# Two attention heads at a time on the two row halves of TensorE, in the expert layers of a four-layer kernel

## The reference

```python
    def _L0_ffn_ref(x, ln1_g, ln1_b, ln2_g, ln2_b, wq, bq, wk, bk, wv, bv, wo, bo, gate_w, gate_b, w1, b1, w2, b2):
        B, S, H, NH, E, F = (4, 128, 128, 16, 8, 512)
        D = H // NH
        ...
        b, s, h = x.shape
        hn = _layernorm(x, ln1_g, ln1_b)
        q = (hn @ wq + bq).reshape(b, s, NH, D).transpose(0, 2, 1, 3)
        ...
        scores = jnp.einsum('bhqd,bhkd->bhqk', q, k) / jnp.sqrt(jnp.float32(D))
        attn = jax.nn.softmax(scores, axis=-1)
        o = jnp.einsum('bhqk,bhkd->bhqd', attn, v)
        o = o.transpose(0, 2, 1, 3).reshape(b, s, h)
        x = x + (o @ wo + bo)
        hn2 = _layernorm(x, ln2_g, ln2_b).reshape(-1, h)
        logits = hn2 @ gate_w + gate_b
        idx = jnp.argmax(logits, axis=-1)
        ...
    x = x + _L0_attn_a_ref(_layernorm(x, axis=-1), ...)
    x = x + _L0_ffn_ref(_layernorm(x, axis=-1), ...)
    x = x + _L0_attn_b_ref(_layernorm(x, axis=-1), ...)
    x = x + _L0_ffn_ref(_layernorm(x, axis=-1), ...)
    return x
```

## Time and profile before

| | us |
|---|---|
| median of 3 runs | 1390.95 (1387.69 to 1395.62) |
| the profiled execution, its own time | 1389.94 |
| its span, first to last instruction | 1388.0 |
| PE busy | 1160.6 (84%) |
| VectorE busy | 982.9 (71%) |
| ScalarE busy | 689.2 (50%) |
| mean granted TensorE clock | 0.908 |

### The profile page before, as it was taken

The page is one execution under the profiler, slowest core; times in us unless marked ns, Lnnn a source line. Parts: engine busy times, 40 slices in busy tenths (PEclk is TensorE's granted clock), DMA queues, the critical chain, the costliest instruction groups (busy, mean ns, idle before and its releaser), DMA issues. The chain is left out here.

```text
span 1388.0 us, 33225 instructions
## 1 busy us (share of the span) xinstructions
PE 1160.6 (84%) x13034; PEld 628.2 (45%) x13034; DVE 982.9 (71%) x2128; ACT 689.2 (50%) x1425; POOL 618.8 (45%) x828
## 2 busy tenths in 40 slices
PE   6746777769999998887787988969988999999885
PEld 2212332323333334864465666656666433333375
DVE  5699999978888984535856665736725688888453
ACT  3843443414776767532452452442441367676744
POOL 2359989964235312531632452442532243342153
PEclk9969889987999999898998878989978799999988
DMA  5288944131241402235132232141132303140223
GB/s 152 115 298 315 344 171 172 56 79 49 45 98 53 118 4 88 66 96 107 29 88 51 44 82 55 31 103 28 32 82 47 72 2 92 44 126 10 86 59 89
DMA packets 132800, 127.65 MB, mean 92 GB/s; under 512 B 86295, under 2 KB 117847, under 8 KB 128122
## 3 DMA queue, kind: packets, MB, share of 16 engines
q1 hardware_dynamic: 124592, 117.65, 30.0%
q0 software_dynamic: 2496, 5.13, 1.2%
q10 hardware_dynamic: 5558, 2.76, 1.0%
HBM read 104.83 MB, written 37.90 MB: 103 GB/s over the span
## 5 line engine op out<-in xcount | busy, mean ns | idle before, releaser
L1480 DVE TENSOR_REDUCE f_row_min<-f_ps 128x1 f32<-128x512 f32 x480 | 308.1, 681 | 54.5 <-PE f_ps L1811 54.0
L1361 ACT ACTIVATE f_e<-f_ps 128x512 f32<-128x512 f32 x512 | 279.1, 598 | 124.9 <-PE f_ps L1830 124.1
L816 PE MATMUL m_ps<-m_shared,sb_ident 128*128 128x512 f32 x256 | 132.5, 663 | 54.9 <-DVE m_shared L664 52.9
L379 POOL TENSOR_TENSOR m_drive<-m_du,m_ring 128x1024 f32<-128x1024 f32 x64 | 149.7, 2354 | 49.0 <-DVE m_ps L656 31.7
L522 ACT ACTIVATE m_ps<-m_delta,m_A 128x511 f32<-128x511 f32 x128 | 82.9, 681 | 117.2 <-DVE m_ps L656 98.3
L1841 PE MATMUL f_ps<-f_e,f_v_op 128*32 128x512 f32 x1024 | 137.3, 608 | 2.4 <-ACT f_e L1361 1.4
L2700 DVE TENSOR_REDUCE d_row_min<-d_ps 128x1 f32<-128x384 f32 (+3 forms) x176 | 104.2, 632 | 23.1 <-PE d_ps L2935 22.0
L816 PEld LDWEIGHTS m_ps<-m_shared,sb_ident 128*128 128x128 f32 x256 | 51.2, 211 | 138.5 <-DVE m_shared L664 81.6
L656 DVE TENSOR_TENSOR_SCAN m_ps<-m_ps,m_drive 128x1024 f32<-128x1024 f32 x44 | 101.1, 2297 | 5.0
L1811 PE MATMUL f_ps<-f_second_ops 72*128 72x512 bf16 x256 | 98.0, 383 | 2.8 <-DVE f_row_min L1480 2.8
L1811 PE MATMUL f_ps<-first_ops 72*128 72x512 bf16 x224 | 92.2, 421 | 8.6 <-DVE f_row_min L1480 6.4
(11 more groups left out here) (319 smaller groups left out, 2305.5 us busy)
## 6 DMA issues: line engine op xcount, KB each, us to landing
m_ring<-bc_scr SPq DMA_DIRECT2D x32, 1024.0 KB, 5.4
f_rows_scr<-blank SPq DMA_DIRECT2D x2, 8707.5 KB, 32.0
f_wall<-f_wall SPq DMA_DIRECT2D x16, 578.0 KB
first_ops<-q_scr SPq DMA_DIRECT2D x28, 288.0 KB
first_ops<-k_scr SPq DMA_DIRECT2D x84, 96.0 KB
f_second_ops<-q_scr SPq DMA_DIRECT2D x16, 288.0 KB
f_second_ops<-k_scr SPq DMA_DIRECT2D x48, 96.0 KB
f_second_ops<-f_rows_scr SPq DMA_DIRECT2D x36, 64.5 KB, 1.8
```

Of the source, the lines that this page charges most:

```text
L379: nc.gpsimd.tensor_tensor(drive[:, step % AHEAD, :].rearrange("p (a s) -> p a s", a=HALVES), du[:, :, tokens(b)], b_row(step).unsqueeze(1) ...
L816: last = nc.tensor.matmul(bank(Y + k), core.ident[:, :], hC[:, k * S:(k + 1) * S], start=False, stop=last_of_batch)
L1361: nc.scalar.activation(e_sb[:, n % 3, hh, :], ps[:, SCORE[(b * UNITS + u) % SCORE_BANKS], :], ACT.Exp, scale=SCALE).then_inc(s["e_out"], 1)
L1480: nc.vector.tensor_reduce(row_min[:, b % 2, u // TPB, u % TPB:u % TPB + 1], ps[:, MAXQ[unit(b, u) % MAX_BANKS], :], AX.X, ALU.max, negate= ...
```

## The change

For batches 1 to 3 of each expert layer (batch 0 stays as it is) a head no longer has its rows at partitions 0 to 71. Two heads are put side by side: head A has 64 of its 72 rows at partitions 0 to 63, head B 64 of its rows at 64 to 127. These 64 rows hold all products of parts but the last, third query part by third key part. That product's 8 rows and the 3 shift rows, 11 rows, stand at the head of the same half, in another slot of the same tensor (`REST_AT` heads further on).

- A maximum uses the 64 rows alone: one matmul per unit as before, on one row half; two units of two heads follow each other (`placed_head`).
- A score becomes two matmuls into one bank: 64 rows, then 11 rows. TensorE's program has, for a pair: 64 rows of A, 64 rows of B, 11 rows of A, 11 rows of B. Only the last one of each tells ScalarE.
- In the whole loop, batch 0 too, two maxima follow each other and then two scores.
- Loading a group of heads takes 12 DMAs (48, 16 and 8 rows, query and key, two halves) instead of 4, with 2 KB pieces instead of 4 KB and the same bytes. A quarter's shifts take two DMAs instead of one, and batch 2 also reloads ones, one DMA per group. On SyncE groups 2 and 3 of a batch are now loaded behind the shifts of quarter 3.

```diff
+HALF = P // 2
+LOW_ROWS = (PARTS - 1) * PARTS * HD
+REST_AT = GROUP // 2
...
                 def load_group(b, g):
                     if b >= 2:
                         sp.wait_ge(s["s_ps"], (b - 2) * UNITS + (g + 1) * GROUP * TPB)
-                    heads = slice(g * GROUP, (g + 1) * GROUP)
-                    sp.dma_start(q_op(b, slice(0, QK_ROWS))[:, heads, :], query_rows(q_scr[stored(b), :, :, heads, :])).then_inc(
-                        op_in[b % 2][g], 16)
-                    load_keys(b, g, heads)
+                    ops = second_ops if b % 2 else core.first_ops
+                    at, rest_at = slice(g * GROUP, g * GROUP + REST_AT), slice(g * GROUP + REST_AT, (g + 1) * GROUP)
+                    for half in range(2):
+                        heads = slice(g * GROUP + half * REST_AT, g * GROUP + (half + 1) * REST_AT)
+                        rows = halves(ops)[half]
+                        for i, (low, high, rest) in enumerate((some_query_rows(q_scr[stored(b), :, :, heads, :]),
+                                                               some_key_rows(k_scr[stored(b), :, :, heads, :]))):
+                            sp.dma_start(rows[0:LOW_ROWS, i, at, :], low).then_inc(op_in[b % 2][g], 16)
+                            sp.dma_start(rows[LOW_ROWS:HALF, i, at, :], high).then_inc(op_in[b % 2][g], 16)
+                            sp.dma_start(rows[0:HD, i, rest_at, :], rest).then_inc(op_in[b % 2][g], 16)
...
                 def for_maximum(b, u):
-                    hd, t, n = u // TPB, u % TPB, unit(b, u)
+                    hd, t, half, slot = placed_head(b, u)
+                    n = unit(b, u)
...
-                    nc.tensor.matmul(ps[:, MAXQ[n % MAX_BANKS], :], q_op(b, QK)[:, hd, t * P:(t + 1) * P],
-                                     k_op(b, QK)[:, hd, :], start=True, stop=True).then_inc(s["max_ps"], 1)
+                    rows, slot = (slice(0, QK_ROWS), hd) if b == 0 else (slice(half * HALF, (half + 1) * HALF), slot)
+                    nc.tensor.matmul(ps[:, MAXQ[n % MAX_BANKS], :], q_op(b, rows)[:, slot, t * P:(t + 1) * P],
+                                     k_op(b, rows)[:, slot, :], start=True, stop=True).then_inc(s["max_ps"], 1)
...
-                    if n >= SCORE_BANKS:
-                        pe.wait_ge(s["e_out"], n - SCORE_BANKS + 1)
-                    hd = g * GROUP + hh
-                    nc.tensor.matmul(ps[:, SCORE[n % SCORE_BANKS], :], k_op(b, QKS)[:, hd, t * P:(t + 1) * P],
-                                     q_op(b, QKS)[:, hd, :], start=True, stop=True).then_inc(s["s_ps"], 1)
+                    cols = slice(t * P, (t + 1) * P)
+                    for p in range(2):
+                        if n + p >= SCORE_BANKS:
+                            pe.wait_ge(s["e_out"], n + p - SCORE_BANKS + 1)
+                        bank = ps[:, SCORE[(n + p) % SCORE_BANKS], :]
+                        if b == 0:
+                            hd = g * GROUP + u % GROUP + p
+                            nc.tensor.matmul(bank, k_op(b, QKS)[:, hd, cols], q_op(b, QKS)[:, hd, :],
+                                             start=True, stop=True).then_inc(s["s_ps"], 1)
+                        else:
+                            rows, slot = slice(p * HALF, (p + 1) * HALF), g * GROUP + u % GROUP // 2
+                            nc.tensor.matmul(bank, k_op(b, rows)[:, slot, cols], q_op(b, rows)[:, slot, :],
+                                             start=True, stop=False)
+                    for p in range(2 if b else 0):
+                        rows, slot = slice(p * HALF, p * HALF + HD + PARTS), g * GROUP + REST_AT + u % GROUP // 2
+                        nc.tensor.matmul(ps[:, SCORE[(n + p) % SCORE_BANKS], :], k_op(b, rows)[:, slot, cols],
+                                         q_op(b, rows)[:, slot, :], start=False, stop=True).then_inc(s["s_ps"], 1)
...
-                    if m < B:
+                    if m < B and mu % 2 == 0:
                         for_maximum(m, mu)
-                    if 0 <= b < B:
-                        score(b, u)
+                        for_maximum(m, mu + 1)
+                    if 0 <= b < B and u % 2 == 0:
+                        scores(b, u)
```

More of the change, by code:

```diff
@@ L933 @@
 STEPS = GROUPS * TPB
+HALF = P // 2
+LOW_ROWS = (PARTS - 1) * PARTS * HD
+REST_AT = GROUP // 2
+HALF_LOADS = 6
 SCORE_BANKS = 3
@@ L1056, in k_op, with halves, in_slots, placed_head @@
             return (second_ops if b % 2 else core.first_ops)[rows, 1]
+        def halves(ops):
+            return [ops[half * HALF:(half + 1) * HALF] for half in range(2)]
+        def in_slots(rows, first):
+            return rows.rearrange("r (g e a) s -> r g e a s", g=GROUPS, e=2)[:, :, first // REST_AT, :, :]
+        def placed_head(b, u):
+            if b == 0:
+                return u // TPB, u % TPB, None, None
+            g, v = divmod(u, GROUP * TPB)
+            a, v = divmod(v, 2 * TPB)
+            return g * GROUP + v % 2 * REST_AT + a, v // 2, v % 2, g * GROUP + a
+        def head_in_group(b, p):
+            return p if b == 0 else p % 2 * REST_AT + p // 2
         skipped_units, skipped_quarters, skipped = (ENTERED, ENTERED_QUARTERS, 1) if entered else (0, 0, 0)
@@ L1067, in shifts_loaded @@
         def shifts_loaded(b, k):
[L1068 removed]
+            return 16 * 2 * (b + 1 - (k < skipped_quarters))
         def operand_loads(b, g):
[L1071 to L1074 removed]
+            first = 0 if b % 2 or entered or g < KEY_GROUPS else PARTS
+            ones = 1 if b == 2 else 0
+            return 16 * (first + ones + 2 * HALF_LOADS * ((b + 1) // 2))
         def prepared_at(m):
@@ L1278, in shifts @@
                     sp.wait_ge(s["m_out"], quarter(b, k) + 1)
-                    sp.dma_start(q_op(b, slice(QK_ROWS, SHIFT_ROWS))[:, quarter_heads(k), :].rearrange("j h (t s) -> j (h t) s", t=TPB),
-                                 max_part[:, k, :]).then_inc(m_in[k], 16)
+                    for half in range(2):
+                        heads = slice(k * GROUP + half * REST_AT, k * GROUP + (half + 1) * REST_AT)
+                        rest_at = slice(k * GROUP + REST_AT, (k + 1) * GROUP)
+                        rows = (q_op(0, slice(QK_ROWS, SHIFT_ROWS))[:, heads, :] if b == 0 else
+                                halves(second_ops if b % 2 else core.first_ops)[half][HD:HD + PARTS, 0, rest_at, :])
+                        sp.dma_start(rows.rearrange("j h (t s) -> j (h t) s", t=TPB),
+                                     max_part[half * PARTS * IN_QUARTER // 2:(half + 1) * PARTS * IN_QUARTER // 2, k, :]).then_inc(
+                            m_in[k], 16)
                 def load_walls(first):
@@ L1291, in _ @@
                         load_keys(0, g, slice(g * GROUP, (g + 1) * GROUP))
-                for o in range(skipped, 2):
-                    sp.dma_start(k_op(o, slice(QK_ROWS, SHIFT_ROWS)),
-                                 core.dram["ones"].rearrange("j (h s) -> j h s", h=NH)).then_inc(s["ones_in"], 16)
+                ones = core.dram["ones"].rearrange("j (h s) -> j h s", h=NH)
+                if not skipped:
+                    sp.dma_start(k_op(0, slice(QK_ROWS, SHIFT_ROWS)), ones).then_inc(s["ones_in"], 16)
+                for rows in halves(second_ops):
+                    sp.dma_start(in_slots(rows[HD:HD + PARTS, 1], REST_AT), in_slots(ones, REST_AT)).then_inc(s["ones_in"], 16)
                 for b in range(B):
@@ L1298, in _ @@
                             shifts(b, k)
-                    if skipped < b + 1 < B:
+                    goes_on = skipped < b + 1 < B
+                    if goes_on:
                         store_parts(b + 1)
-                        for g in range(GROUPS // 2):
-                            load_group(b + 1, g)
-                    shifts(b, 2)
-                    if skipped < b + 1 < B:
-                        for g in range(GROUPS // 2, GROUPS):
-                            load_group(b + 1, g)
-                    shifts(b, 3)
+                        load_group(b + 1, 0)
+                    shifts(b, 2)
+                    if goes_on:
+                        load_group(b + 1, 1)
+                    shifts(b, 3)
+                    for g in range(2, GROUPS):
+                        if goes_on:
+                            load_group(b + 1, g)
                     if b >= 1:
@@ L1816, in turn_maxima, with scores @@
                     pe.wait_ge(*side_free("maxima", b, k))
-                    nc.tensor.matmul(ps[0:PARTS * IN_QUARTER, SIDE, 0:P], min_part[:, :, :].rearrange("p j r -> p (j r)"),
+                    nc.tensor.matmul(ps[0:PARTS * IN_QUARTER, SIDE, 0:P], min_part[:, :, :, :].rearrange("p e j r -> p (e j r)"),
                                      w["ident_b"], start=True, stop=True).then_inc(s["mT_ps"], 1)
-                def score(b, u):
-                    q, hh, n = u // GROUP, u % GROUP, b * UNITS + u
+                def scores(b, u):
+                    q, n = u // GROUP, b * UNITS + u
```

42 lines of the change are left out of this document (26 added, 16 removed).

## The result

The changed kernel takes 1432.94 us (median, 1427.49 to 1441.03), the kernel before beside it 1390.98: a ratio of 1.0323, 95% interval 1.0277 to 1.0368. That is 42 us slower; the forecast was 1424, its range 1392 to 1465. The profiled executions differ by 1427.49 - 1389.94 = 37.6, where the sum of the prediction has 34.8. The mean granted clock is 0.908 in both.

A forecast was written before the change was run, and what follows sets the result against it. TensorE was taken to bound the kernel. Per layer 17.2 - 8.3 + 2.3 + 5.2 + 1 = 17.4 us, twice 34.8, added to 1389.94 gave 1424.7, stated as 1424, with a range of 1392 to 1465.

The forecast's parts named there:

- Overlap: Pairs of matmuls on different row halves stream together, 0.22 us for two instead of 0.44, the second starting 0.03 later.
- tile change: On TensorE, each change between 64-row and 32-row tiles costs 0.09 us, within bounds of 0 and 0.16.
- loop: A pair's second score waits for ScalarE to free its bank: 1.39 us; clean step 3.27 against 2.84, end step 3.05.
- free changes: Rival: changing between 64-row and 32-row tiles on TensorE costs nothing; step 3.10 us, time 1400; chance 0.09.
- the loop doesn't hold TensorE back: Rival: results reach ScalarE sooner or the second score's bank is free when asked; step 2.52 to 2.76, time 1370; chance 0.09.
- 40 x 0.43, -8.3, 2.3, 5.2, 1: Terms in us per layer: steps beside maxima, waits filled by blocks, other blocks' tile changes, end steps, batch 0; sum 17.4.
- the term of 0.43 a step: Each of 40 score steps beside maxima in a layer becomes 0.43 us longer, 3.27 against 2.84; 17.2 per layer.
- Ten blocks at 0.09: Ten blocks of other work per batch each add one tile change of 0.09 us; 2.3 per layer.
- SyncE hidden in layer 3: In the second expert layer, four groups of loads at 5.4 us each end before quarter 2's shifts are wanted; no cost.
- the fourth rival: Rival: the forecast plus SyncE late, every issue costing 0.87 us, some 11 late in the second expert layer; 1437; chance 0.06.
- Groups 2 and 3, now behind quarter 3's shifts: nothing: On SyncE, these loads are wanted 32 and 48 units after their batch starts, so moving them costs nothing.
- TensorE sets the pace: In the kernel before, from batch 1's scores to batch 2's, TensorE is busy 55.69 of 57.82 us and is the bound.

The follow-up runs named there:

- e2: Changed kernel with both heads of a pair on rows 0 to 63, so no two matmuls overlap, and a smaller exponential scale; 1660.77 us.
- e1: Changed kernel with each 11-row matmul replaced by a second pass over the same 64 rows, and a smaller exponential scale; 1421.46 us, ratio 1.026.
- e10: Changed kernel with VectorE's maximum and, from the fourth step on, ScalarE's exponential reading 64 of 512 columns; 1398.38 us, ratio 1.009.
- e11: Kernel before with VectorE's maximum and ScalarE's exponential cut to 64 of 512 columns, the control of e10; 1363.47 us, ratio 0.983.
- e7: Changed kernel with batch 0's shifts issued ahead of the loads of groups 2 and 3 in the second expert layer; 1439.01 us, ratio 1.038.
- e5: Changed kernel with ScalarE's exponentials on 256 of 512 columns from the fourth step on; 1431.16 us, ratio 1.033.
- e9: Changed kernel unaltered, run again on the chip of e10 to e12; 1448.85 us, ratio 1.047 to the kernel before.
- e6: Kernel before with ScalarE's exponentials on half of the columns from the fourth step on; 1380.19 us, ratio 0.997.
- e3: Changed kernel with maxima still packed but each score one matmul of 75 rows, and a smaller exponential scale; 1406.11 us, ratio 1.015.
- e12: Changed kernel with the second 64-row pass of e1 and the 64-column readers of e10; 1381.73 us, ratio 0.996.

## Why the prediction was right

- **Overlap, tile change, loop.** Two 64-row matmuls stream in the time of one, the second at most 0.01 behind, not 0.03 (e2 without the overlap: 3.99 a step, as worked out). The change between 64 and 32 rows is 0.09, as taken; e1 removes it. The loop through ScalarE is 1.45 for 1.39, the clean step 3.30 for 3.27, the end step 3.10 for 3.05. The rivals "free changes" and "the loop doesn't hold TensorE back" fall; the second would have needed readers that e10 had to shorten to an eighth.
- **40 x 0.43, -8.3, 2.3, 5.2, 1.** In sum 17.4 against 16.8 in layer 1. That it comes so close is partly luck, as single terms are off in both directions. Batch 1 lost less (3.4 for 4.5): the kernel before already waited there, 3.2 us by e11, of which 0.8 ahead of its products, and the term of 0.43 a step takes a step without waits as the base. Batch 3 lost less (6.1 and 0.8 for 7.4). Batches 0 and 2 lost half a us more, in batch 2 through the wait of batch 3's first score.
- **Ten blocks at 0.09: mis-sized.** Leaving a 128-row tile costs more than going into a 32-column one: 0.59 for 0.43 at the turns, 0.99 for 0.81 at the logits, 1.3 us over batch 1's blocks where the term has 0.9, and 1.8 between e10 and e11. The Trainium skill, "TensorEngine Tiling (Array Packing)", Key Properties, has it that changing the tiling mode drains TensorE, with no figure; these runs agree, and the price depends on what is left: 0.09 from 64 rows to 32, 0.16 to 0.18 out of a block.
- **SyncE hidden in layer 3: this step failed.** I drew a line through issues of 3, 24 and 72 rows and read 0.38 for 16 rows; it is 0.60 to 0.70. A group is 7.1 to 7.2 us instead of 5.4, four of them and the ones put the shifts past their time, and batch 0 waits 3.5 us; e7 takes 3.9 us off by their order alone. It was the fourth rival's mechanism, at a third of its price.
- **"Groups 2 and 3, now behind quarter 3's shifts: nothing": this failed too.** I looked at when these loads are wanted and not at what stands behind them on SyncE, batch 3's first shifts. It costs 0.7 and 0.5 us in the changed kernel, and up to 3.3 us in the variants whose batches are shorter (e5).
- **The clock: "I expect 2.4 GHz to stay".** True in batch 1 of every run but e2, and in the first profile from batch 1 on. Not true in others: in e9 TensorE stands for 2 to 3 us and then has 7 and 17 us at 1.2 GHz. In the profiles this is 16.3 of the 19.1 us between two executions of the same kernel, and the likely difference between 1.032 and 1.047 on two chips. It is one reason why e5 and e7 can't be judged by their totals. I had given it no share; it belonged in the range's upper part.
- **"TensorE sets the pace"** was only mostly true: e11 shows 3.2 us of waits for readers in 57.8. Exponentials half as long take off 0.4 alone (e6), so most of it probably hangs on VectorE; no run shortened VectorE's reader alone.

None of the versions beats the kernel before; those that come under it leave work out. None gave the scores a fourth bank, which the account of the loop would call for.

## What to carry to other kernels

Before packing matmuls two by two, follow one bank around its ring: matmul start to reader start, reader start to bank free, the rest of the pair, and compare that with TensorE's own work between two pairs. A pair asks for a bank one unit earlier than single matmuls do, and with three banks that closed the ring (1.39 against 0.88 us) and turned a saving of 0.14 a step into a loss of 0.46. Compare a stretch at the same granted clock, here one batch that repeats to 0.1 us, before judging an edit by the total. And where a queue gets more issues, look at everything that stands behind them in it, a whole batch on: in e1, e3, e5 and e12, whose batches are shorter, that wait grew.
